# A graph layer on one core: five whole groups of gathered rows brought by SyncE, a place transfer issued from ScalarE, and the rows of v laid out in the table's order

## The chip, the cores and the metric

The kernel runs on one core of one Trainium2 chip. The time is device microseconds of one execution; three runs of the kernel before gave a median of 1986.8 us. Five engines work side by side and meet at semaphores: TensorE (PE, matmul), VectorE (DVE), ScalarE (ACT), GpSimd (POOL) and SyncE (SP). SP and ACT can issue direct DMA transfers, whose addresses may come out of a register; POOL issues the indirect ones, which take a column of 128 row numbers and bring 128 rows.

## The reference

For 6250 nodes with 64 features and 200000 edges sorted by target node `dst`:

```python
h   = relu(layernorm(x))
p1  = tanh(h @ pp_W1 + pp_b1) @ pp_W2 + pp_b2
e   = concat([p1[src], p1[dst]]) @ pi_W1 + pi_b1      # per edge
e   = ((e @ pi_W2 + pi_b2) @ pi_W3).reshape(E, 64, 8)
i1  = einsum('ecb,eb->ec', e, edge_attr)
i1  = tanh(i1 @ ii_W1 + ii_b1) @ ii_W2 + ii_b2
out = x + segment_sum(i1, dst, num_segments=6250)
```

Since nothing nonlinear stands between `p1` and the einsum, the kernel keeps two tables in DRAM: `u_tab` (a row of 64 float32 per node, for the side of `src`) and `v_tab` (a row of 3 x 64 bfloat16 per node, three parts whose sum is the float32 row, for the side of `dst`).

## The kernel before

The edges are cut into 391 groups (`NG`) of 512: four tiles of 128 edges; the last group, 390, holds 320 edges. After a prologue of about 70 us that makes the tables, every engine walks the groups in the same order, one pass per group, a few passes apart from each other.

- **PE** sums both sides for the group (`newest()`, line 1423): `sum_v` (line 1346) multiplies a one-hot matrix by a window of `v_tab`, and `place_rows` (line 1362) adds the gathered rows of u. Then it spreads the edge features (line 1371), multiplies (line 1379), transposes (line 1386) and adds up by target (line 1474), each for a group one to three passes older. The first 32 passes and the last 30 odd are written out; the passes between run in loops of 8, cut around each group that SP brings.
- **POOL** gathers the rows of u (line 568), four indirect transfers for a group, for groups 7 to 390 without those in `BY_SP`. For groups up to 31 there is a buffer each. From group 40 on it reuses 8 buffers (`UR`), so group g waits until pass g - 8 has used its rows (`s_ready`).
- **SP** has in each pass g (line 470): a wait until pass g - 4 has made its one-hot matrix and `load_loc(g)` (line 415), the places of the edges in their window, broadcast to 126 partitions, 126 KB; a wait until pass g - 4 is summed and the window of v (line 479), 42 table rows of 3 x 64 values, 15.8 KB, to 126 partitions, at a register address; every 16th pass the next source numbers and edge features; and in a stretch of passes `fetch_rows`, four single rows of u of 256 B at register addresses (line 440), for which it first reads four row numbers into registers (line 436). Every 8th pass it reads eight window starts into registers (line 472), with a bounds check on each. Three passes before the group is due, `place_fetched` (line 448) copies the staged rows to the place where PE takes them, in four transfers.
- **ACT** copies the sums out (`make_s`, line 756, four instructions), then does the tanh (line 744) and a copy (line 747) for the group two passes older (`make_t`).
- **DVE** makes the one-hot matrices (lines 1051 and 1094) and the products (line 987).

`BY_SP` names the groups that SP brings, the pass in which it begins, and over how many passes (one partition of four rows a pass):

```python
BY_SP = [(135, 4, P), (263, 132, P), (NG - 1, 260, PART)]
```

So SP brings groups 135, 263 and 390, 1344 rows, in passes 4 to 339. A window row of v for node n and part w lies on partition 42 w + n (`n w d -> w n d`), and the one-hot matrix compares with `iota_p`, which holds the partition modulo 42.

Of the kernel before, what the change touches and what calls it, by code (L numbers as in the profile page):

```python
# [8 lines left out]
def program(nc, x, src, dst, edge_attr, pp_W1, pp_b1, pp_W2, pp_b2, pi_W1, pi_b1, pi_W2, pi_b2, pi_W3,  # L9
# [6 lines left out]
    P = 128  # L16
# [59 lines left out]
    UNITS = [(k, min(2, XG - k)) for k in range(0, XG, 2)]  # L76
    EARLY_V = 4

    BY_SP = [(135, 4, P), (263, 132, P), (NG - 1, 260, PART)]

    assert EPP * NP == EARLY and LPP * NP == N - EARLY and LPP == 10 and Y_STEP + 4 * BATCHES < NG + 4
    assert NP * NPP == N and PART * TILES + FULL * GE == E and F == FC * P and NG <= PIECE * PIECES
# [4 lines left out]
    with ctx:  # L87
# [17 lines left out]
        ident = sb("ident", [P, P])  # L105
        ident_b = sb("ident_b", [P, P], bf16)
        iota_f = sb("iota_f", [P, BW])
        iota_i = sb("iota_i", [P, 2], i32)
        iota_p = sb("iota_p", [P, 3])
        iota_8 = sb("iota_8", [P, 1])  # L110
        spread = sb("spread", [P, NB, D], bf16)
        g_sb = sb("g_sb", [P, FC, D])
# [4 lines left out]

        u_rows = sb("u_rows", [P, UR, TILES, D])
        sp_stage = sb("sp_stage", [P, 2, TILES, D])
        sp_idx = sb("sp_idx", [P, len(BY_SP) * TILES], i32)  # L120
        v_win = sb("v_win", [3 * W, VR, D], bf16)
        loc_bc = sb("loc_bc", [P, VR, GE], bf16)
        hot_t = sb("hot_t", [3 * W, 2, GE], bf16)
# [201 lines left out]
        def has(g):  # L325
            return 0 <= g < NG
# [8 lines left out]
        def _(sp):  # L335
# [90 lines left out]
            oe = out[0:EARLY, :].rearrange("(p i) d -> p (i d)", i=EPP)  # L426

            def load_sp_idx():
                for k, (g, _, n) in enumerate(BY_SP):
                    sp.dma_start(sp_idx[0:n, k * TILES:(k + 1) * TILES],  # L430
                                 src[g * GE:g * GE + n * TILES].rearrange("(p j) -> p j", j=TILES)
                                 ).then_inc(sp_idx_in, 16)

            def fetch_rows(k, p):

                _, at = nc.values_load_multi_w_load_instructions(
                    sp_idx[p:p + 1, k * TILES:(k + 1) * TILES], engines=[mybir.EngineType.SP], min_val=0, max_val=N - 1,
                    skip_runtime_bounds_check_because="src names nodes of x")
                for j in range(TILES):
                    sp.dma_start(sp_stage[p:p + 1, k % 2, j, :], u_tab[bass.ds(at[j], 1), :]  # L440
                                 ).then_inc(sp_rows_in[k], 16)

            def place_fetched(k):

                g, _, n = BY_SP[k]
                sp.wait_ge(sp_rows_in[k], 16 * TILES * n)
                for j in range(TILES):
                    sp.dma_start(u_rows[:, g % UR, j, :], sp_stage[:, k % 2, j, :]).then_inc(fetched[k], 16)

            def store_early(lo, hi):  # L450
                cols = slice(lo * D, hi * D)
# [12 lines left out]
            with sp.If(is_fast):  # L464
                store_v()
                for g in range(VR):
                    load_loc(g)
                v_landed()
                load_sp_idx()
                for g in range(NG):  # L470
                    if g % 8 == 0:
                        _, starts = nc.values_load_multi_w_load_instructions(  # L472
                            base_row[0:1, g:min(g + 8, NG)], engines=[mybir.EngineType.SP], min_val=0, max_val=N - W)
                    start = starts[g % 8]
                    if g >= VR:
                        sp.wait_ge(hot_t_ready, g - VR + 1)
                        load_loc(g)
                        sp.wait_ge(s_ready, g - VR + 1)
                    sp.dma_start(v_win[:, g % VR, :], v_tab[bass.ds(start, W), :, :].rearrange("n w d -> w n d")
                                 ).then_inc(v_in[g % VR], 16)  # L480
                    k = g // PIECE + 2
                    if g % PIECE == 0 and k < PIECES:
                        if k >= LD:
                            sp.wait_ge(part1, k - LD + 1)
                        load_src(k)
                        load_basis(k)
                    if g == (PIECES - 2) * PIECE:
                        load_last()
                    if g == PIECE // 2:
                        load_x()  # L490
                    if g == BY_SP[0][1]:
                        sp.wait_ge(sp_idx_in, 16 * len(BY_SP))
                    for k, (of, first_at, n) in enumerate(BY_SP):
                        if k >= 2 and g == first_at:
                            sp.wait_ge(s_ready, BY_SP[k - 2][0] + 1)
                        if 0 <= g - first_at < n:
                            fetch_rows(k, g - first_at)
                        if g == of - 3:
                            place_fetched(k)
                    if g == NG - 6:  # L500
                        sp.wait_ge(y_ready, 4)
                        store_early(0, 4 * SLICE)
                store_rest()
# [20 lines left out]
        def _(pool):  # L524
# [31 lines left out]
            with pool.If(is_fast):  # L556
                pool.wait_ge(u_stored, 32 * NC)
                pool.wait_ge(ld[0], ld_count(0))
                for g in range(XG, NG):
                    k = g // PIECE  # L560
                    if g % PIECE == 0:
                        pool.wait_ge(ld[k % LD], ld_count(k))
                    if g in [of for of, _, _ in BY_SP]:
                        continue
                    if g >= AHEAD + UR:
                        pool.wait_ge(s_ready, g - UR + 1)
                    for j in range(TILES):
                        pool.indirect_dma_start(  # L568
                            out=u_rows[:, g % UR, j, :] if g >= AHEAD else first_u[:, g - XG, j, :],
                            out_offset=None, in_=u_tab[:, :],  # L570
                            in_offset=bass.IndirectOffsetOnAxis(
                                ap=src_e[:, g * TILES + j:g * TILES + j + 1].bitcast(u32), axis=0),
                        ).then_inc(u_in[g % UR] if g >= AHEAD else first_u_in[g - XG], 16)
# [20 lines left out]
        def _(act):  # L594
# [155 lines left out]
            def copy_st(r):  # L750
# [6 lines left out]
                            "p (q a e) -> p q a e", q=2, a=TILES), ACT.Identity, bias=s_bias[part, 0:1])  # L757
                return last

            def make_s(n):  # L760
                act.wait_ge(s_ready, n + 1)
                if has(n - 2):
                    act.wait_ge(o_ready, n - 1)
                copy_st(n % 2).then_inc(st_ready, 1)
# [16 lines left out]
            with act.If(is_fast):  # L781
                zero_upper()
                root_rows()
                place_columns()
                zero_lower()
                relu_rows(0)
                for k in range(1, len(UNITS)):
                    relu_rows(k)
                    tanh_rows(k - 1)
                tanh_rows(len(UNITS) - 1)  # L790
                for n in STEPS:
                    if has(n) and n < TURN:
                        make_s(n)
                    if has(n - 2):
                        make_t(n - 2)
                    if has(n) and n >= TURN:
                        make_s(n)
                store_rest()
# [15 lines left out]
        def _(dve):  # L814
# [61 lines left out]
            norm(4)  # L876
            dve.wait_ge(consts, 1)
            nc.vector.tensor_copy(ident_b[:], ident[:])
            nc.vector.tensor_copy(iota_p[:, 0:1], iota_i[:, 0:1])
            nc.vector.tensor_scalar(iota_i[:, 1:2], iota_i[:, 0:1], NB - 1, None, ALU.bitwise_and)  # L880
            dve.drain()
            for k in (1, 2):
                nc.vector.tensor_scalar(iota_p[:, k:k + 1], iota_p[:, 0:1], float(k * W), float(W), ALU.is_ge,
                                        ALU.mult)
            nc.vector.tensor_copy(iota_8[:], iota_i[:, 1:2])
            dve.drain()
            nc.vector.tensor_tensor(iota_p[:, 1:2], iota_p[:, 1:2], iota_p[:, 2:3], ALU.add)

            u_copy(0)
            dve.wait_ge(rows_in, 48)  # L890
# [16 lines left out]
            nc.vector.tensor_tensor(iota_p[:, 0:1], iota_p[:, 0:1], iota_p[:, 1:2], ALU.subtract)  # L907
# [276 lines left out]
        def _(pe):  # L1184
# [226 lines left out]
            skipped = [of for of, _, _ in BY_SP]  # L1411

            def step(n, u, first, last_pass, g=None, fetched_pass=False, gone=(0,) * UN):

# [8 lines left out]
                def newest():  # L1423
# [10 lines left out]
                        place_rows(first_u[:, g - XG, :, :], False).then_inc(s_ready, 1)  # L1434
                    else:
                        if fetched_pass and n + u in skipped:
                            pe.wait_ge(fetched[skipped.index(n + u)], 16 * TILES)
# [45 lines left out]
            with pe.If(is_fast):  # L1483
# [9 lines left out]
                    step(g - g % UN, g % UN, g < UN, False, g)  # L1493
                gone = [0] * UN
                at = AHEAD
                for of in skipped[:-1]:
                    with pe.Fori(at, of // UN * UN, UN) as n:
                        for u in range(UN):
                            step(n, u, False, False, gone=gone)
# [5 lines left out]
                with pe.Fori(at, LOOP_END, UN) as n:  # L1505
                    for u in range(UN):
                        step(n, u, False, False, gone=gone)
                for n in range(LOOP_END, NG + 5, UN):
                    for u in range(UN):
                        step(n, u, False, True, fetched_pass=True, gone=gone)  # L1510
                pe.wait_ge(acc_done, NG)
                y_late()
            with pe.Else():
# [48 lines left out]
```

## Time and profile before

| what | value |
|---|---|
| median of 3 runs (lowest to highest) | 1986.8 us (1985.95 to 1989.17) |
| the profiled execution's own time | 1983.09 us |
| its span, first to last instruction | 1981.2 us |
| busy PE, POOL, DVE, ACT | 1733.1, 1479.1, 1449.0, 1109.5 us |
| mean granted TensorE clock | 0.963 |

The profile is of one execution. Its span is 1.9 us shorter than its own time and its time is 3.7 us below the median. A busy time does not count the issuing of DMA transfers, so SP has none; what SP does is read from the timeline of its queue. POOL's gathers count as busy for about 0.94 us each, with 0.3 us from one to the next.

### The profile page before, as it was taken

The numbers are of one execution on the slowest core, as the hardware profiler recorded it, in microseconds if no ns is written. First come the engines' busy times: TensorE is split into PE (matmuls) and PEld (weight loads), VectorE is DVE, ScalarE is ACT, GpSimd is POOL, SyncE is SP. The second block draws the span as 40 slices with busy tenths as digits, with TensorE's granted clock in tenths as the row PEclk, the third lists the DMA queues.
The fourth block names the chain that finished last, engine by engine and source line by source line (L and its number), as shares of the span: only waits on it lengthen the run. The fifth ranks groups of instructions, "written<-read, shape, count | busy, mean of one in ns | idle before, by whom it ended". The sixth has DMA issues, their size and how long they took to land.

```text
span 1981.2 us, 58993 instructions
## 1 busy us (share of the span) xinstructions
PE 1733.1 (87%) x20012; PEld 1134.5 (57%) x20012; DVE 1449.0 (73%) x1939; ACT 1109.5 (56%) x2419; POOL 1479.1 (75%) x1569
## 2 busy tenths in 40 slices
PE   7699999989988898888888888888888888888998
PEld 6466566655555555555555555555555555555666
DVE  7688778877677777677777777677777767777766
ACT  5666656655555555555555555555555555555554
POOL 7777777777777777777777777777777777777773
PEclk9799999999899999999999999899999999999999
DMA  6543333333333332332333323333233233332331
GB/s 141 115 82 62 67 67 64 61 65 66 58 63 58 62 66 56 63 62 56 62 55 61 62 56 60 61 63 64 55 63 62 56 59 62 59 59 54 59 71 44
DMA packets 266170, 127.83 MB, mean 65 GB/s; under 512 B 188169, under 2 KB 238328, under 8 KB 265864
## 3 DMA queue, kind: packets, MB, share of 16 engines
q1 hardware_dynamic: 214767, 74.86, 17.9%
q0 software_dynamic: 49664, 50.96, 15.4%
q14 instruction: 134, 1.10, 0.2%
q8 instruction: 47, 0.77, 0.2%
q10 hardware_dynamic: 1558, 0.15, 0.1%
HBM read 119.42 MB, written 6.00 MB: 63 GB/s over the span
## 4 chain that ended last, share of the span: by engine, by line
POOL 62%; issue 21%; PE 11%; ACT 2%; DMA 1%; SPq 1%; DVE 1%; ACTq 0%; DVEq 0%; POOLq 0%
POOL u_rows L568 62%; PE bank L1379 5%; PE bank L1474 1%; PE bank L1362 1%; DMA loc_bc<-loc_tab 1%; PE bank L1386 1%; PE spread_ps L1371 1%; DVE o_sb L987 1%; PE bank L1346 1%; ACT st_sb L756 0%; SPq L472 0%; SPq L440 0%; PE spread_ps L1208 0%; PE bank L1356 0%; DMA v_tab<-acc_all 0%
## 5 line engine op out<-in xcount | busy, mean ns | idle before, releaser
L568 POOL DMA_INDIRECT u_rows<-u_tab,src_e x1424 | 1352.4, 950 | 434.1 <-issue 433.1
L987 DVE TENSOR_TENSOR o_sb<-st_sb,spread_ps 128x2048 f32<-128x2048 f32 x391 | 892.9, 2284 | 365.0 <-PE spread_ps L1371 346.8
L756 ACT ACTIVATE st_sb<-bank,s_bias 64x256 f32<-64x256 f32 x1564 | 734.3, 469 | 438.0 <-PE bank L1362 406.9
L1379 PE MATMUL bank<-o_sb,g_sb 128*64 128x256 f32 x6256 | 807.0, 403 | 1.0 <-DVE o_sb L987 0.8
L1379 PEld LDWEIGHTS bank<-o_sb,g_sb 128*64 128x64 f32 x6256 | 433.5, 143 | 232.9 <-issue 36.7
L1362 PE MATMUL bank<-ident,u_rows 128*128 128x128 f32 x1436 | 259.3, 304 | 191.9 <-DMA u_rows<-u_tab,src_e 191.0
L1051 DVE TENSOR_TENSOR hot_t<-loc_bc,bank 126x512 bf16<-126x512 bf16 x391 | 268.8, 688 | 144.0 <-PE bank L1474 59.7
L1362 PEld LDWEIGHTS bank<-ident,u_rows 128*128 128x128 f32 x1436 | 189.8, 192 | 240.5 <-DMA u_rows<-u_tab,src_e 228.0
L1474 PEld LDWEIGHTS bank<-hot,t_sb 128*65 128x65 f32 x3128 | 216.1, 139 | 158.6 <-issue 150.6
L744 ACT ACTIVATE tt_sb<-bank,z_bias 128x256 f32<-128x256 f32 x391 | 185.4, 474 | 175.1 <-PE bank L1379 174.4
L1474 PE MATMUL bank<-hot,t_sb 128*65 128x42 f32 x3128 | 262.8, 235 | 9.1 <-DVE acc_all L1100 8.6
L747 ACT COPY t_sb<-bank 128x256 f32<-128x256 f32 x391 | 146.5, 375 | 221.8 <-PE bank L1386 218.1
L1386 PE MATMUL bank<-ident,tt_sb 128*128 128x128 f32 x782 | 170.4, 300 | 0.6 <-ACT tt_sb L744 0.6
L1371 PE MATMUL spread_ps<-bt_sb,spread 24*128 24x128 bf16 x6256 | 161.0, 221 | 5.0 <-DVE o_sb L987 4.8
L1346 PE MATMUL bank<-hot_t,v_win 126*64 126x128 bf16 x1564 | 118.4, 231 | 12.0 <-issue 7.7
L1094 DVE TENSOR_TENSOR hot<-loc_e,bank 128x168 f32<-128x168 f32 x391 | 125.9, 322 | 0.0
L1371 PEld LDWEIGHTS spread_ps<-bt_sb,spread 24*128 24x128 bf16 x6256 | 92.6, 94 | 54.1 <-issue 6.4
L568 POOL DMA_INDIRECT basis<-u_tab,src_e x100 | 96.4, 964 | 31.9 <-issue 30.2
L1346 PEld LDWEIGHTS bank<-hot_t,v_win 126*64 126x64 bf16 x1564 | 56.1, 108 | 79.1 <-issue 78.5
L1386 PEld LDWEIGHTS bank<-ident,tt_sb 128*128 128x128 f32 x782 | 79.7, 142 | 35.5 <-ACT tt_sb L744 1.4
L1100 DVE TENSOR_TENSOR acc_all<-acc_all,bank 65x42 f32 x391 | 72.9, 186 | 3.5 <-PE bank L1474 3.5
L1035 DVE STREAM_TRANSPOSE bt_sb<-b_parts 128x512 bf16<-128x512 bf16 x98 | 68.5, 699 | 0.0
(148 smaller groups left out, 353.3 us busy)
## 6 DMA issues: line engine op xcount, KB each, us to landing
loc_bc<-loc_tab SPq DMA_DIRECT2D x391, 126.0 KB
u_rows<-u_tab,src_e POOLq DMA_INDIRECT x1424
sp_stage<-u_tab SPq DMA_DIRECT2D x1344, 0.2 KB
v_win<-v_tab SPq DMA_DIRECT2D x391, 15.8 KB
basis<-edge_attr SPq DMA_DIRECT2D x24, 256.0 KB, 4.2
v_tab<-acc_all SPq DMA_DIRECT2D x6, 336.0 KB
basis<-u_tab,src_e POOLq DMA_INDIRECT x100, 2.7
u_tab<-basis SPq DMA_DIRECT2D x6, 224.0 KB
```

The source lines that it names most:

```text
L568: pool.indirect_dma_start(out=u_rows[:, g % UR, j, :] if g >= AHEAD else first_u[:, g - XG, j, :], out_offset=None, in_=u_tab[:, :], in_of ...
L744: return nc.scalar.activation(tt_sb[:, r, :], z_ps, ACT.Tanh, bias=z_bias[:, 0:1])
L747: return nc.scalar.copy(t_sb[:, r, :, 0:D].rearrange("p (h q) c -> p q h c", h=2), t_ps.rearrange("p (q h c) -> p q h c", q=2, h=2))
L756: last = nc.scalar.activation(tiles[h * D:(h + 1) * D, j], s_ps[part].rearrange("p (q a e) -> p q a e", q=2, a=TILES), ACT.Identity, bias= ...
L987: return nc.vector.tensor_tensor(o_sb[:, r, :, :].rearrange("p c (j e) -> p j c e", j=TILES), st_sb[:, r, :].rearrange("p (j e) -> p j e", ...
L1051: nc.vector.tensor_tensor(hot_t[:, g % 2, :], loc_bc[0:3 * W, g % VR, :], pick_ps.to_broadcast([3 * W, GE]), ALU.is_equal).then_inc(hot_t_ ...
L1346: nc.tensor.matmul(s_ps[TWICE[j], q * P:(q + 1) * P].rearrange("k (a e) -> k a e", a=TILES), v_win[:, u % VR, :], hot_t[:, u % 2, :].rearr ...
L1362: last = nc.tensor.matmul(s_ps[:, q * P:(q + 1) * P], rows[:, 2 * q:2 * q + 2, :].rearrange("p j k -> p (j k)"), ident[:], start=alone and ...
L1371: last = nc.tensor.matmul(spread_ps[:, a, c * P:(c + 1) * P], spread[q, 2 * c:2 * c + 2, :].rearrange("p b k -> p (b k)"), bt_sb[q, r, :], ...
L1379: last = nc.tensor.matmul(z_ps[h * D:(h + 1) * D, 0:2 * P], g_sb[:, c, :], o_sb[:, r, c, 2 * h * P:(2 * h + 2) * P], start=(c == 0), stop= ...
L1386: last = nc.tensor.transpose(t_ps[:, q * P:(q + 1) * P], tt_sb[:, r, q * P:(q + 1) * P], ident[:])
L1474: last = nc.tensor.matmul(seg_ps, t_sb[:, (u - 3) % 2, j, :], hot[:, (u - 3) % HR, j, :], start=(j == 0), stop=(j == TILES - 1))
```

## The change

SP brings five whole groups, 83, 157, 231, 305 and 380, seven rows a pass, each over 74 passes (4 to 77, 78 to 151 and so on to 373). The row numbers of a group lie in one partition and are read eight at a time. The copy to the place where PE takes them is one transfer. POOL gathers the 320-edge last group, which SP brought before. `load_loc` moves from SP's queue to ACT's, behind `make_s`; ACT issues it for the group four passes on. The window of v lands in the order of the table (partition 3 n + w), so that its source is one run of rows, and `iota_p` holds the partition divided by 3. The bounds check on the window starts is left out. PE's loops are cut around four groups instead of two.

```diff
-    BY_SP = [(135, 4, P), (263, 132, P), (NG - 1, 260, PART)]
+    ROWS = 7
+    BY_SP = [(83, 4), (157, 78), (231, 152), (305, 226), (380, 300)]
+    AT_ONCE = 8
...
-        sp_idx = sb("sp_idx", [P, len(BY_SP) * TILES], i32)
+        sp_idx = sb("sp_idx", [1, len(BY_SP) * GE], i32)
...
             def load_sp_idx():
-                for k, (g, _, n) in enumerate(BY_SP):
-                    sp.dma_start(sp_idx[0:n, k * TILES:(k + 1) * TILES],
-                                 src[g * GE:g * GE + n * TILES].rearrange("(p j) -> p j", j=TILES)
+                for k, (g, _) in enumerate(BY_SP):
+                    sp.dma_start(sp_idx[0:1, k * GE:(k + 1) * GE], row(src[g * GE:(g + 1) * GE])
                                  ).then_inc(sp_idx_in, 16)
-            def fetch_rows(k, p):
-
-                _, at = nc.values_load_multi_w_load_instructions(
-                    sp_idx[p:p + 1, k * TILES:(k + 1) * TILES], engines=[mybir.EngineType.SP], min_val=0, max_val=N - 1,
-                    skip_runtime_bounds_check_because="src names nodes of x")
-                for j in range(TILES):
-                    sp.dma_start(sp_stage[p:p + 1, k % 2, j, :], u_tab[bass.ds(at[j], 1), :]
+            def fetch_rows(k, rows, at):
+
+                for r in rows:
+                    p, j = divmod(r, TILES)
+                    if r % AT_ONCE == 0:
+                        _, at = nc.values_load_multi_w_load_instructions(
+                            sp_idx[0:1, k * GE + r:k * GE + r + AT_ONCE], engines=[mybir.EngineType.SP], min_val=0,
+                            max_val=N - 1, skip_runtime_bounds_check_because="src names nodes of x")
+                    sp.dma_start(sp_stage[p:p + 1, k % 2, j, :], u_tab[bass.ds(at[r % AT_ONCE], 1), :]
                                  ).then_inc(sp_rows_in[k], 16)
+                return at
             def place_fetched(k):
-                g, _, n = BY_SP[k]
-                sp.wait_ge(sp_rows_in[k], 16 * TILES * n)
-                for j in range(TILES):
-                    sp.dma_start(u_rows[:, g % UR, j, :], sp_stage[:, k % 2, j, :]).then_inc(fetched[k], 16)
+                g, _ = BY_SP[k]
+                sp.wait_ge(sp_rows_in[k], 16 * GE)
+                sp.dma_start(u_rows[:, g % UR, :, :], sp_stage[:, k % 2, :, :]).then_inc(fetched[k], 16)
...
                         _, starts = nc.values_load_multi_w_load_instructions(
-                            base_row[0:1, g:min(g + 8, NG)], engines=[mybir.EngineType.SP], min_val=0, max_val=N - W)
+                            base_row[0:1, g:min(g + 8, NG)], engines=[mybir.EngineType.SP], min_val=0, max_val=N - W,
+                            skip_runtime_bounds_check_because="VectorE made them from dst and cut them at N - W")
                     start = starts[g % 8]
                     if g >= VR:
-                        sp.wait_ge(hot_t_ready, g - VR + 1)
-                        load_loc(g)
                         sp.wait_ge(s_ready, g - VR + 1)
-                    sp.dma_start(v_win[:, g % VR, :], v_tab[bass.ds(start, W), :, :].rearrange("n w d -> w n d")
+                    sp.dma_start(v_win[:, g % VR, :], v_tab[bass.ds(start, W), :, :].rearrange("n w d -> (n w) d")
                                  ).then_inc(v_in[g % VR], 16)
...
-                        if 0 <= g - first_at < n:
-                            fetch_rows(k, g - first_at)
+                        if first_at <= g:
+                            at = fetch_rows(k, range(ROWS * (g - first_at), min(ROWS * (g - first_at + 1), GE)), at)
...
+            def load_loc(g):
+                act.wait_ge(hot_t_ready, g - VR + 1)
+                act.dma_start(loc_bc[0:3 * W, g % VR, :], loc_tab[g:g + 1, :].to_broadcast([3 * W, GE])
+                              ).then_inc(loc_in[g % VR], 16)
...
                 for n in STEPS:
                     if has(n) and n < TURN:
                         make_s(n)
+                    if has(n + VR):
+                        load_loc(n + VR)
                     if has(n - 2):
                         make_t(n - 2)
...
-            nc.vector.tensor_copy(iota_p[:, 0:1], iota_i[:, 0:1])
             nc.vector.tensor_scalar(iota_i[:, 1:2], iota_i[:, 0:1], NB - 1, None, ALU.bitwise_and)
+            nc.vector.tensor_scalar(iota_i[:, 2:3], iota_i[:, 0:1], 171, None, ALU.mult)
             dve.drain()
-            for k in (1, 2):
-                nc.vector.tensor_scalar(iota_p[:, k:k + 1], iota_p[:, 0:1], float(k * W), float(W), ALU.is_ge,
-                                        ALU.mult)
+            nc.vector.tensor_scalar(iota_i[:, 0:1], iota_i[:, 2:3], 9, None, ALU.logical_shift_right)
...
-                for of in skipped[:-1]:
+                for of in [of for of in skipped if of < LOOP_END]:
                     with pe.Fori(at, of // UN * UN, UN) as n:
```

## Rows read from the trace of the kernel before

**Rows 1.** The page's part 4: the chain that ended last, by engine.

```profile
POOL 62%; issue 21%; PE 11%; ACT 2%; DMA 1%; SPq 1%; DVE 1%; ACTq 0%; DVEq 0%; POOLq 0%
```

**Rows 2.** Line 568: duration ns min/median/max, first and last start; idle until; landing.

```profile
L568 POOL DMA_INDIRECT u_rows<-u_tab,src_e x1424: 940/944/1532, 169.2 to 1954.5; - x178
L568 POOL DMA_INDIRECT basis<-u_tab,src_e x100: 940/944/1365, 42.4 to 168.0; - x100
...
  PE bank L1362: 0.9, 3
...
DMA to landing us min/median/max: 2.4/2.7/4.7
```

**Rows 3.** The chain that ended last, 1840 to 1982 us: start, length, what.

```profile
1919.51 4.69 DMA u_rows<-u_tab,src_e
...
1965.41 0.66 PE bank L1362 x4
```

**Rows 4.** Timeline of SP's queue, 140 to 165 us: start, length, line, transfer.

```profile
140.66 1.49 SPq L440 DMA_DIRECT2D sp_stage<-u_tab  x4
142.20 0.32 SPq L415 DMA_DIRECT2D loc_bc<-loc_tab  x1
142.71 0.75 SPq L479 DMA_DIRECT2D v_win<-v_tab  x1
144.50 1.50 SPq L440 DMA_DIRECT2D sp_stage<-u_tab  x4
...
160.32 1.52 SPq L440 DMA_DIRECT2D sp_stage<-u_tab  x4
164.76 0.35 SPq L415 DMA_DIRECT2D loc_bc<-loc_tab  x1
```

**Rows 5.** SP's instructions by line, whole span: duration ns min/median/max.

```profile
L440 SPq DMA_DIRECT2D sp_stage<-u_tab x1344: 224/225/465, 75.0 to 1691.6; - x192
L436 SPq TENSOR_LOAD <-sp_idx x336: 497/814/923, 74.0 to 1689.4; - x168
L472 SPq TENSOR_LOAD <-base_row x49: 689/783/1445, 60.6 to 1910.3; - x49
L479 SPq DMA_DIRECT2D v_win<-v_tab x391: 722/749/936, 64.0 to 1945.2; - x196
L415 SPq DMA_DIRECT2D loc_bc<-loc_tab x391: 311/320/1253, 55.5 to 1941.6; - x196
L448 SPq DMA_DIRECT2D u_rows<-sp_stage x12: 555/601/610, 658.1 to 1934.9; - x12
```

**Rows 6.** Waits of SP's queue, whole span: us in total, times, longest.

```profile
SPq L479 <- PE bank L1362: 294.7, 190, 5.1
```

**Rows 7.** Timeline of SP's queue, 60 to 240 us: the windows of passes 4, 17, 33.

```profile
73.22 0.76 SPq L479 DMA_DIRECT2D v_win<-v_tab  x1
...
134.98 0.78 SPq L479 DMA_DIRECT2D v_win<-v_tab  x1
...
205.11 0.77 SPq L479 DMA_DIRECT2D v_win<-v_tab  x1
```

**Rows 8.** Timelines of PE (passes 3 and 33) and POOL (group 41 begins).

```profile
84.85 0.30 PE L1346 MATMUL bank<-hot_t,v_win 126*64 126x128 bf16 x4
...
209.83 0.30 PE L1346 MATMUL bank<-hot_t,v_win 126*64 126x128 bf16 x4
...
214.17 0.94 POOL L568 DMA_INDIRECT u_rows<-u_tab,src_e  x1 [0.30 <-issue]
```

**Rows 9.** ACT and DVE near 701 us; line 1082 on DVE's queue; a transfer issued by ACT.

```profile
700.53 1.92 ACT L756 ACTIVATE st_sb<-bank,s_bias 64x256 f32<-64x256 f32 x4 [0.50 <-PE bank L1362]
702.75 0.47 ACT L744 ACTIVATE tt_sb<-bank,z_bias 128x256 f32<-128x256 f32 x1 [0.31 <-PE bank L1379]
...
701.12 2.29 DVE L987 TENSOR_TENSOR o_sb<-st_sb,spread_ps 128x2048 f32<-128x2048 f32 x1 [0.80 <-PE spread_ps L1371]
...
L1082 DVEq TENSOR_LOAD <-base_row x1: 320/320/320, 701.1 to 701.1; - x1
...
L602 ACTq DMA_DIRECT2D wraw<-L_gnn_pi_W x1: 665/665/665, 1.9 to 1.9; - x1
```

More of the change, by code:

```diff
@@ L107, in program @@
         iota_f = sb("iota_f", [P, BW])
-        iota_i = sb("iota_i", [P, 2], i32)
-        iota_p = sb("iota_p", [P, 3])
+        iota_i = sb("iota_i", [P, 3], i32)
+        iota_p = sb("iota_p", [P, 1])
         iota_8 = sb("iota_8", [P, 1])
@@ L469, in _ @@
                 load_sp_idx()
+                at = None
                 for g in range(NG):
@@ L492, in _ @@
                         sp.wait_ge(sp_idx_in, 16 * len(BY_SP))
-                    for k, (of, first_at, n) in enumerate(BY_SP):
+                    for k, (of, first_at) in enumerate(BY_SP):
                         if k >= 2 and g == first_at:
                             sp.wait_ge(s_ready, BY_SP[k - 2][0] + 1)
-                        if 0 <= g - first_at < n:
-                            fetch_rows(k, g - first_at)
+                        if first_at <= g:
+                            at = fetch_rows(k, range(ROWS * (g - first_at), min(ROWS * (g - first_at + 1), GE)), at)
                         if g == of - 3:
@@ L560, in _ @@
                     k = g // PIECE
+                    if g == FULL:
+                        pool.wait_ge(last_in, 32)
                     if g % PIECE == 0:
                         pool.wait_ge(ld[k % LD], ld_count(k))
-                    if g in [of for of, _, _ in BY_SP]:
+                    if g in [of for of, _ in BY_SP]:
                         continue
@@ L878, in _ @@
             nc.vector.tensor_copy(ident_b[:], ident[:])
-            nc.vector.tensor_copy(iota_p[:, 0:1], iota_i[:, 0:1])
             nc.vector.tensor_scalar(iota_i[:, 1:2], iota_i[:, 0:1], NB - 1, None, ALU.bitwise_and)
+            nc.vector.tensor_scalar(iota_i[:, 2:3], iota_i[:, 0:1], 171, None, ALU.mult)
             dve.drain()
-            for k in (1, 2):
-                nc.vector.tensor_scalar(iota_p[:, k:k + 1], iota_p[:, 0:1], float(k * W), float(W), ALU.is_ge,
-                                        ALU.mult)
+            nc.vector.tensor_scalar(iota_i[:, 0:1], iota_i[:, 2:3], 9, None, ALU.logical_shift_right)
             nc.vector.tensor_copy(iota_8[:], iota_i[:, 1:2])
             dve.drain()
-            nc.vector.tensor_tensor(iota_p[:, 1:2], iota_p[:, 1:2], iota_p[:, 2:3], ALU.add)
+            nc.vector.tensor_copy(iota_p[:], iota_i[:, 0:1])
             u_copy(0)
@@ L906, in _ @@
                                     ).then_inc(rows_done, 1)
-            nc.vector.tensor_tensor(iota_p[:, 0:1], iota_p[:, 0:1], iota_p[:, 1:2], ALU.subtract)
             u_copy(3)
@@ L1409, in y_late @@
                     last.then_inc(y_ps, 1)
-            skipped = [of for of, _, _ in BY_SP]
+            skipped = [of for of, _ in BY_SP]
             def step(n, u, first, last_pass, g=None, fetched_pass=False, gone=(0,) * UN):
@@ L1436, in newest @@
                         if fetched_pass and n + u in skipped:
-                            pe.wait_ge(fetched[skipped.index(n + u)], 16 * TILES)
+                            pe.wait_ge(fetched[skipped.index(n + u)], 16)
                         else:
@@ L1504, in _ @@
                     at += UN
-                with pe.Fori(at, LOOP_END, UN) as n:
-                    for u in range(UN):
-                        step(n, u, False, False, gone=gone)
+                if at < LOOP_END:
+                    with pe.Fori(at, LOOP_END, UN) as n:
+                        for u in range(UN):
+                            step(n, u, False, False, gone=gone)
                 for n in range(LOOP_END, NG + 5, UN):
@@ L1510, in _ @@
                         step(n, u, False, True, fetched_pass=True, gone=gone)
+                        if n + u in skipped:
+                            gone[u] += 1
                 pe.wait_ge(acc_done, NG)
```

## The prediction, made before the changed kernel had run

> **What bounds the kernel now.** I read the chain that ended last first, because the shares of busy time name PE (1733 us) while PE spends much of its time waiting. The chain goes to POOL for 62%, and most of its "issue" is the 0.3 us between two of POOL's gathers [rows 1]. The view of line 568 tells why: 1524 gathers, the first at 42.4 and the last at 1954.5 us, so one every (1954.5 - 42.4) / 1523 = 1.2555 us, and all of POOL's waiting for PE is 0.9 us [rows 2]. POOL never rests from its first gather to its last. A group costs it 4 x 1.2555 = 5.02 us; PE, where nothing holds it, needs 4.1 us a pass (30 passes from pass 3 to pass 33 took 125 us [rows 8], some of them already late). So POOL's early lead over PE is eaten up, and from then on PE runs at POOL's pace.
>
> The end of the chain must be read apart. POOL's last gather, of group 389, is not on it: the chain leaves POOL at the gather that starts at 1919.51, 28 gathers before the last, which is the last one of group 382; PE then runs eight more passes by itself, and the end comes 61.7 us after that gather [rows 2, 3].
>
> SP is the second limit. Its pass is read off its queue's timeline [rows 4, 5]: the four rows take 1.49 us from first start to last end with 0.225 each, so one row every 0.42 us. From the end of the v transfer to the first row it is 1.04 us; without the reading of the row numbers it would be the 0.20 between two rows, so reading costs 0.84. The places cost 0.32 + 0.055, v 0.19 + 0.75. Sum: 4 x 0.42 + 0.84 + 0.375 + 0.94 = 3.84. From v of pass 17 to v of pass 33 are 70.13 us, 4.38 a pass [rows 7]; the 0.54 more is two readings of the window starts, the 16-pass transfers and small delays. Over the whole run SP still waits 294.7 us for PE [rows 6].
>
> **What each part costs or gives.**
>
> *POOL.* Five whole groups leave it instead of two whole ones and the last, so it gathers 379 groups instead of 381: 8 x 1.2555 = 10.0 us less in all. The path, however, leaves POOL at group 382. Before that group two had been skipped, now five: 12 gathers less, 15.1 us, so the gather at 1919.51 moves to 1904.4. With the same 61.7 us behind it the span ends at 1966.1. A check from the other side: group 390 is now POOL's. Its last gather starts 32 gathers after 1904.4, at 1944.6; 2.7 us to landing [rows 2] gives 1947.3, and from the sum of the last group (1965.41) to the end are 15.8 us [rows 3]: 1963. So POOL's own last gather would just not be the later one. The landing on the chain took 4.69 where 2.7 is usual; with a usual one the end comes 2 us earlier. 1963 to 1970 is what this part leaves open; I take 1966.
>
> *SP's pass.* Rows: 512 / 74 = 6.92 a pass x 0.42 = 2.91. Reading eight numbers is not shown for these numbers, but eight window starts take 0.783 in one instruction against 0.814 for four row numbers [rows 5], so a reading costs the same 0.84, now 64 in 74 passes: 0.73. The places leave. The starts without their bounds check: every eighth pass 2.9 us go by between row and places (161.84 to 164.76), of which the reading is 0.78; the checks cost 2.05 each eighth pass, 0.26 a pass, and the 0.54 of other work becomes 0.28. The copy to the place is one transfer instead of four of 0.6 and costs nothing beside that.
>
> The v transfer is the open price. Its new form (126 destination partitions, one run of rows in DRAM) is not in the trace. Upper bound: the old 0.749. Lower bound: the places' transfer, which goes to the same 126 partitions with eight times the bytes in 0.320 [rows 5]. I take 0.32, the row nearest in shape, and keep 0.75. The pass is then 2.91 + 0.73 + 0.19 + 0.32 + 0.28 = 4.43, or 4.86 with the old price. The trace shows two transfers to 126 partitions with more than twofold different issue times [rows 5]. The Trainium skill (DMA: Bandwidth & Descriptors, Why a DMA increments its semaphore by 16 and not by 1) says that the engines a transfer runs on are the largest number up to 16 that divides both sides' slowest dimension: by it the old v, whose source has 3 in front, runs on 3 and the new one on 14, as the places do. By that rule the sum is the one with 0.32; a reader who sets the rule aside has 4.43 to 4.86.
>
> Does 4.43 suffice? In the long run yes: POOL's pace is 5.02 x 73 / 74 = 4.95 a pass. The same by totals: 1216 more rows x 0.42 = +511, 387 places gone -145, bounds checks -100, readings -13, v -168 gives +85 us out of 294.7 of slack; with the old v +253, which leaves some 42.
>
> The beginning is tighter, because there PE runs ahead of 4.95 and POOL's 8 buffers tie it to PE: group 41 may start when pass 33 is summed. It started at 214.17; pass 33 began at 209.83 and its sum takes about 0.95, so 3.4 us were spare [rows 8]. How late is v of pass 33 now? From pass 4 to 33, 29 passes: rows +3 x 0.42 x 29 = +36.5; readings -0.125 x 0.84 x 29 = -3.0; places -10.9; v -12.5; four bounds checks -8.2: +1.9 us, so it is issued at 207.0 instead of 205.1. With 0.32 and a landing of 2.7 (the gathers'; v's own is not shown) pass 33 can begin at 210.0, as before. No stall. With the old v it is issued at 219.5, pass 33 is summed near 223.9, and POOL loses 9.7 us.
>
> *ACT.* It issues 387 transfers that SP issued at 0.32 and that ACT could issue at up to 0.67 [rows 9]. The wait in front is met already: the sums that `make_s` has just copied needed the same one-hot matrix. I count it at nothing, since ACT's queue can issue while its four copies of 1.92 us run; the trace shows that for DVE, whose queue reads a window start at 701.1 while its 2.29 us product runs [rows 9]. If the cover is gone, the tanh, which idles 0.31 us for PE, comes 0.67 - 0.31 = 0.36 later, and PE's transposes with it. In exchange the places come from a queue that is not busy. This removes waits of DVE, but not on the path that sets the end.
>
> *The rest.* Two more transfers of row numbers (about 0.9 us on SP) stand ahead of pass 0, with 2 us of checks gone in the same place. DVE's constants are a few tiny instructions on either side. PE has 16 more passes written out, and the first 32, written out too, run at 4.1. I add nothing.
>
> **The sum.** The profiled execution's span becomes 1966.1 (15.1 less), its own time 1.9 more, 1968.0; the median of the runs lay 3.7 above the profiled time: 1971.7, say 1972 us, 0.7% less.
>
> **The rivals.**
>
> *A: v's issue stays at 0.75.* For: no row shows the new form. Against: the row of the places. POOL stalls 9.7 us early, SP at 4.86 stays just inside 4.95: 1971.7 + 9.7 = 1981, 0.3% faster. It bites from a v of 0.32 + 3.4 / 30 = 0.43 on.
>
> *B: ACT's issue is not hidden.* PE's free pass becomes 4.1 + 0.36; pass 33 begins at 84.85 + 30 x 4.46 = 218.7 and is summed at 219.6, so POOL stalls 5.4 us at group 41; the eleven passes from 380 to 390 add 4. 1971.7 + 9.4 = 1981. Against: DVE's row.
>
> *C, slower: the single rows choke.* SP sends 1.56 rows per us instead of 4 / 4.38 = 0.91, each a transfer of its own. If they back up, a row costs more than 0.42 and SP becomes the bound: pass 373 can begin no sooner than 73.2 + 369 s. POOL brings group 373 by 1904.4 - 8 x 5.02 = 1864, so s up to about 4.86 is free; the 15 us of gain are gone at 4.90, which is a row of 0.49. At 0.52 s is 5.12, which is (5.12 - 4.86) x 369 = 96 us over the forecast: 2068. Against: 1344 rows at a median of 225 ns, never over 465, four in a row at 0.42 [rows 5]. The skill's same page and section says that a transfer of one row runs on one engine, the lowest-numbered one, which speaks against 2560 of them; no row here shows which engine took them.
>
> *D: nothing gained at the end,* if PE, not POOL, sets the last passes from group 380 on. But it comes out of group 380 with one skipped group as lead and needs about 4.2 where POOL needs 5.02; that loses at most the 4 us up to 1970. The time would be 1976.
>
> **How the numbers follow.** Forecast 0.68 (1966 to 1977, with stalls of a few us inside it), A 0.11, B 0.11, C 0.08, the rest better than forecast. Within 0.2% (1982.8 to 1990.8) is about what a measurement of this kernel can tell from no change. A and B lie just below its edge, half of each in it. So faster 0.80, same 0.11, slower 0.09. The range is 1965 to 1985: it leaves out C and the dearer ends of A and B.
>
> **What would show it.** Line 440: 2560 rows at 225 ns, 0.42 apart. Line 479 near 0.32. SP's wait for PE near 210 us. POOL's last gather at 1944 to 1945 and its waiting for PE under 2 us; 5 to 10 us there is A or B. ACT's tanh still 0.3 us behind the copies where PE is free: else B. The chain leaving POOL in the last ten groups. The prediction is wrong if SP's queue stands on the chain after 300 us.

## The result, and the profile after

| | before | after |
|---|---|---|
| median of 4 runs (lowest to highest) | 1986.97 us (1985.95 to 1989.17) | 1971.34 us (1966.45 to 1973.25) |
| ratio to before, 95% interval | | 0.9916 [0.9896, 0.9937] |
| the profiled execution's own time; its span | 1983.09; 1981.2 us | 1972.48; 1970.7 us |
| mean granted TensorE clock | 0.963 | 0.969 |

The kernel is 0.8% faster, and the interval lies wholly below no change. The forecast was 1972. The span that it was built on was 1966.1, though, and the span is 1970.7: 4.6 us of the sum were missed. The median was taken to lie 3.7 us above the profiled execution's time, and this time it lies 1.1 below it. The two misses cancel by luck, so the close agreement of the totals says less than the agreement of the steps.

First the page's part 4 of the changed kernel, the chain that ended last, by engine [rows 1]:

```profile
POOL 55%; issue 21%; PE 11%; SPq 9%; DMA 1%; ACT 1%; DVE 0%; ACTq 0%; POOLq 0%; DVEq 0%
```

POOL still leads. SP's queue, at 1% before, has 9%. Now POOL's gathers, line 573 (duration ns min/median/max, first and last start; then idle until; landing) [rows 2]:

```profile
L573 POOL DMA_INDIRECT u_rows<-u_tab,src_e x1416: 943/947/1496, 169.7 to 1948.5; - x177
L573 POOL DMA_INDIRECT basis<-u_tab,src_e x100: 943/947/1452, 42.5 to 168.5; - x100
...
  PE bank L1371: 1.2, 4
...
DMA to landing us min/median/max: 2.4/2.9/5.0
```

1516 gathers instead of 1524, and again no rest: the waiting for PE is 1.2 us in four pieces, and each piece is no more than the 0.3 us that lie between any two gathers. The pace is (1948.5 - 42.5) / 1515 = 1.2581 us instead of 1.2555.

Instructions of SP and ACT by line, whole span (duration ns min/median/max) [rows 5]:

```profile
L443 SPq DMA_DIRECT2D sp_stage<-u_tab x2560: 224/228/2403, 74.9 to 1853.1; - x197
L440 SPq TENSOR_LOAD <-sp_idx x320: 687/783/949, 74.0 to 1848.4; - x160
L482 SPq DMA_DIRECT2D v_win<-v_tab x391: 321/322/1177, 63.0 to 1934.4; - x196
L451 SPq DMA_DIRECT2D u_rows<-sp_stage x5: 490/492/1099, 415.0 to 1872.2; - x5
L767 ACTq DMA_DIRECT2D loc_bc<-loc_tab x387: 313/314/636, 73.5 to 1934.3; - x194
```

The row kept its price. The window of v fell from 749 to 322 ns, the lower of the prediction's two bounds. Waits of SP's queue [rows 6]:

```profile
SPq L482 <- PE bank L1371: 207.8, 174, 6.1
```

The chain that ended last, from 200 to 446 us (start, length, what), around passes 33 and 34 and where POOL takes over [rows 7, 8]:

```profile
200.82 1.06 SPq L358
...
202.06 2.40 SPq L443
...
207.98 1.70 DMA v_win<-v_tab
...
209.91 0.30 PE bank L1355 x4
...
215.95 0.64 PE bank L1371 x4
...
437.39 3.27 DMA v_win<-v_tab
440.70 0.30 PE bank L1355 x4
441.00 0.66 PE bank L1371 x4
441.91 0.95 POOL u_rows L573
```

Up to 437 us SP's queue stands on the chain again and again, but nothing is lost there: v of pass 33 is issued at 207.98 and pass 33 begins at 209.91, 0.08 later than before, and POOL does not wait. Two of POOL's gathers, the first of group 42 and the first of group 87 (timeline of POOL; in brackets the idle time before):

```profile
220.29 0.95 POOL L573 DMA_INDIRECT u_rows<-u_tab,src_e  x1 [0.30 <-issue]
...
441.91 0.95 POOL L573 DMA_INDIRECT u_rows<-u_tab,src_e  x1 [0.30 <-PE bank L1371]
```

and the sum of pass 79 (timeline of PE; the passes are counted by their sums):

```profile
414.58 0.71 PE L1371 MATMUL bank<-ident,u_rows 128*128 128x128 f32 x4
```

Group 42 needs pass 34, which is summed at 215.95 + 0.64 = 216.59. With the usual 0.30 us between gathers it could have begun at 216.89, so 3.4 us were spare. That is the least of any group that reuses a buffer. Group 87 needs pass 79, summed at 415.29 at the latest, so 26 us were spare at 441.91. The page names PE as what released that gather only because the sum of a later pass, 85, ended inside the ordinary 0.3 us. So the link by which the chain comes from SP's queue to POOL is no delay, and the 9% do not say that SP's queue held anything up.

The chain at the end [rows 3]:

```profile
1893.40 3.64 DMA u_rows<-u_tab,src_e
1897.08 1.23 PE bank L1371 x4
...
1903.13 0.64 PE bank L1371 x4
...
1936.45 0.53 PE bank L1403 x7
...
1954.59 0.66 PE bank L1371 x4
```

The chain leaves POOL 44 gathers before the last, at group 378, not 382. PE then runs to the sum of group 390 in 57.5 us, 13 steps of 4.42 on average (12 groups and one step without a sum). In most of these steps it also transposes rows of the output (line 1403, 0.53 us).

### The profile page after: what moved, and what is told of

It is laid out like the page before. It is cut to its first block, busy times and chain, and to the rows that moved or that the text cites. A ratio compares the mean times of both kernels' runs of the same rounds, so it can differ in the third digit from the quotient of the medians.

```text
span 1970.7 us, 61801 instructions
## 1 busy us (share of the span) xinstructions
PE 1717.0 (87%) x20012; PEld 1125.7 (57%) x20012; DVE 1453.4 (74%) x1937; ACT 1109.4 (56%) x2419; POOL 1474.1 (75%) x1561
## 4 chain that ended last, share of the span: by engine, by line
POOL 55%; issue 21%; PE 11%; SPq 9%; DMA 1%; ACT 1%; DVE 0%; ACTq 0%; POOLq 0%; DVEq 0%
POOL u_rows L573 55%; SPq L443 6%; PE bank L1388 4%; SPq L440 2%; PE bank L1371 1%; PE bank L1483 1%; SPq L482 1%; PE bank L1395 1%; PE spread_ps L1380 1%; PE bank L1355 1%; DMA p<-L_gnn_pi_W 0%; DMA v_win<-v_tab 0%; PE spread_ps L1217 0%; DMA u_rows<-u_tab,src_e 0%; PE bank L1223 0%
## 5 line engine op out<-in xcount | busy, mean ns | idle before, releaser
L1388 PE MATMUL bank<-o_sb,g_sb 128*64 128x256 f32 x6256 | 792.4, 397 | 1.0 <-DVE o_sb L996 0.8
L1388 PEld LDWEIGHTS bank<-o_sb,g_sb 128*64 128x64 f32 x6256 | 427.3, 140 | 225.2 <-issue 23.9
```

Source lines behind the costliest of these rows:

```text
L1388: last = nc.tensor.matmul(z_ps[h * D:(h + 1) * D, 0:2 * P], g_sb[:, c, :], o_sb[:, r, c, 2 * h * P:(2 * h + 2) * P], start=(c == 0), stop= ...
```

## The experiments

Each diff is against the changed kernel. Every kernel computes the whole reference. The chips differed by up to 6 us in the kernel before, so kernels are compared by their ratio to it on the same chip; a time given behind a ratio is the ratio times 1986.97.

**e1: v's window in its old order, all else changed.**

```diff
-                    ... v_tab[bass.ds(start, W), :, :].rearrange("n w d -> (n w) d")
+                    ... v_tab[bass.ds(start, W), :, :].rearrange("n w d -> w n d")
```

The lines that make `iota_p` go back with it.

> The changed kernel with v's old order in SBUF (three parts of 42 partitions), all else as changed. The theory (POOL's gathers set the end as long as SP's pass stays below POOL's 4.95 us and POOL has 3 to 4 us to spare at group 41): v's issue goes back from 0.322 to 0.75, SP's pass from the measured 4.53 to 4.96, pass 33 comes some 12 us later, POOL waits 8 to 12 us for PE early on and SP's waiting for PE falls from 208 to about 40 us or less: 1980 to 1990 us. Rival, that the layout matters little because SP had slack anyway: under 1975. Rival, that the issue time hangs on the bytes and not on the pattern: v's issue stays near 0.32.

Measured: 1.009 [1.0073, 1.0107], 2004.9 us, slower than before. The expectation was missed. SP's windows of passes 4 and 373, the first and the last in which it brings rows (timeline of its queue):

```profile
69.97 0.73 SPq L482 DMA_DIRECT2D v_win<-v_tab  x1
...
1898.73 0.74 SPq L482 DMA_DIRECT2D v_win<-v_tab  x1
```

That is (1898.73 - 69.97) / 369 = 4.956 a pass, and from 240 us to the last row no window waits for PE. Its waits for a sum over the whole span, below, all lie after 1905 us:

```profile
SPq L482 <- PE bank L1374: 40.9, 13, 3.6
```

PE waits for these windows instead (waits of PE in e1), 181.8 us where the changed kernel has 8.9:

```profile
PE bank L1358 <- DMA v_win<-v_tab: 181.8, 189, 4.4
```

So SP sets the pace as long as it brings rows. The issue of v (median 757 ns) was as assumed; the pass around it is 0.10 longer than the 4.86 of the prediction. Rival A called that "just inside". By rival C's own formula a pass of 4.956 costs (4.956 - 4.86) x 369 = 35 us over the forecast: 2007, beside the 2004.9.

**e4: the rows alone.** Old order of v, the places on SP, the bounds checks kept: the edits of e1, e2 and e3 in one kernel.

> Only the five groups at seven rows a pass: v's old order, the places on SP and the checks kept. POOL has the same 8 gathers less than before. The theory: SP's pass is 2.91 + 0.73 + 0.375 + 0.94 + 0.54 + 0.1 = 5.6 us, SP becomes the bound up to pass 373: 73 + 369 x 5.6 + 98 for the rest = 2240 us, 2180 to 2260 with SP's waits near nothing. Rival, that POOL sets the end whatever SP does: 1971 to 1985.

Measured: 1.1291 [1.1269, 1.1314], 2243.5 us. Windows of passes 4 and 373, timeline of SP's queue:

```profile
73.10 0.76 SPq L483 DMA_DIRECT2D v_win<-v_tab  x1
...
2137.30 0.75 SPq L483 DMA_DIRECT2D v_win<-v_tab  x1
```

5.594 a pass; the formula gives 1971.7 + 0.734 x 369 = 2242.6. POOL waits 291.2 us for PE, and the chain has SP's queue for 71%. Without the relief of SP the five groups lose 13%.

**e2: the places back on SP.**

```diff
                     if g >= VR:
+                        sp.wait_ge(hot_t_ready, g - VR + 1)
+                        load_loc(g)
                         sp.wait_ge(s_ready, g - VR + 1)
...
-                    if has(n + VR):
-                        load_loc(n + VR)
```

> The changed kernel with the places' transfer back on SP, with its wait, all else as changed. The theory: SP's pass +0.37, 4.90 us; pass 33 comes 10 us later, POOL waits 6 to 8 us early, SP's slack falls from 208 to about 60 us: 1976 to 1984 us. Rival, that moving the places to ACT gave nothing since DVE waited only 44 us for them: 1971, POOL waits under 2 us.

Measured: 0.9982 [0.9973, 0.9992], 1983.4 us. **e3: the bounds checks kept**, without the last argument of the reading at line 476.

> The changed kernel with the bounds check on the window starts kept, all else as changed. The theory: 2.05 us more every eighth pass, 100 us in all out of 208 of slack, pass 33 some 8 us later of which 3.7 are spare: POOL waits 4 to 5 us, 1973 to 1979 us. Rival, that 0.26 us a pass is lost in the slack: 1971, POOL waits under 2 us.

Measured: 0.994 [0.9923, 0.9957], 1975.0 us. **e6: eight rows a pass**, `ROWS = 8`, same groups.

> The changed kernel with eight rows a pass instead of seven: the same five groups, the same 2560 rows, the same gathers, fetched in 64 passes of each 74, so that SP rests in the other ten. The theory, that the early tie counts and not the sum: SP's pass is 5.06 while it fetches, pass 33 comes 15 us later, POOL waits 9 to 13 us early, and SP is level with POOL's pace after that: 1980 to 1988 us. Rival, that only SP's total counts: 1971.

Measured: 0.9965 [0.9951, 0.9979], 1980.0 us. These three are read together. POOL's waiting for PE from 160 to 250 us (idle us, times), first e2:

```profile
  PE bank L1371: 16.6, 3
```

then e3:

```profile
  PE bank L1370: 6.3, 3
```

then e6:

```profile
  PE bank L1371: 9.4, 4
```

In the changed kernel there is no such line in this stretch; in e1 it has 13.1 us. Later, e2, e3 and e6 have only the ordinary 0.3 a time (e1 has up to 1.3). So the stall is where the prediction looked for it, at POOL's first reuse of its buffers, and nowhere else. In e3 it was somewhat larger than the 4 to 5 us expected. In e2, where 6 to 8 us were expected, it was more than twice that. The expectation priced only the longer pass of SP. But the places come late there too, behind SP's rows, and DVE waits for them (waits of DVE in e2), which it did for 44.1 us before and does not at all in the changed kernel:

```profile
DVE hot_t L1060 <- DMA loc_bc<-loc_tab: 344.0, 239, 5.2
```

How much of the 16.6 us is theirs was not taken apart. Against the changed kernel's 0.9916 the three lose 13, 5 and 10 us, about what POOL waits. (The interval of e3 overlaps that of the changed kernel, so there the 6.3 us of waiting are the firmer number.) SP's waiting over the whole span does not tell it. In e6:

```profile
SPq L482 <- PE bank L1371: 222.0, 61, 5.5
```

That is more slack than the changed kernel's 207.8, in a kernel that is 10 us slower: SP has it late, and POOL lost its time early.

**e5: two groups only, with all of SP's relief.**

```diff
-    ROWS = 7
-    BY_SP = [(83, 4), (157, 78), (231, 152), (305, 226), (380, 300)]
+    ROWS = 4
+    BY_SP = [(135, 4), (263, 132)]
```

> The changed kernel with only two groups, 135 and 263, brought by SP at four rows a pass; all that relieves SP stays. POOL gathers 382 groups, 12 gathers more than the changed kernel and 4 more than the kernel before. The theory, that only the number of gathers pays: 12 x 1.256 = 15 us more than the changed kernel, 1984 to 1990 us, though SP waits for PE over 400 us. Rival, that the relief of SP and the earlier places pay by themselves: under 1980.

Measured: 0.9989 [0.998, 0.9998], 14.5 us behind the changed kernel, where 12 gathers at 1.2555 make 15.1. SP waits 1027.5 us there:

```profile
SPq L482 <- PE bank L1371: 1027.5, 364, 5.9
```

With all that slack, the rest of the change, without fewer gathers ahead of the tail, moves the time by 0.1%. The gain is POOL's gathers.

**e7: ACT issues the places twice**, in two transfers of 63 partitions.

```diff
-                act.dma_start(loc_bc[0:3 * W, g % VR, :], loc_tab[g:g + 1, :].to_broadcast([3 * W, GE])
-                              ).then_inc(loc_in[g % VR], 16)
+                for half in (slice(0, 63), slice(63, 126)):
+                    act.dma_start(loc_bc[half, g % VR, :], loc_tab[g:g + 1, :].to_broadcast([63, GE])
+                                 ).then_inc(loc_in[g % VR], 16)
```

SP's four transfers ahead of the loop are cut likewise, and DVE waits for twice the count.

> The changed kernel with the places' transfer cut into two of 63 partitions, so that ACT issues twice as often with the same bytes. The theory, that ACT's queue issues while its copies run: two issues of 0.3 still fit beside 1.92 us, the tanh still starts 0.31 after the copies, PE's free pass stays 4.10: 1969 to 1974 us. Rival, that ACT's issue is on the path: PE's free pass 4.1 + 0.3 to 0.4, POOL waits 4 to 8 us: 1977 to 1982.

Measured: 0.991 [0.9889, 0.9931], no cost within the interval. Timeline of ACT in e7 near 131 us (start, length, engine, line; in brackets the idle time before):

```profile
130.55 0.47 ACT L762 ACTIVATE st_sb<-bank,s_bias 64x256 f32<-64x256 f32 x1 [0.50 <-PE bank L1373]
130.56 0.65 ACTq L769 DMA_DIRECT2D loc_bc<-loc_tab  x2
131.04 1.44 ACT L762 ACTIVATE st_sb<-bank,s_bias 64x256 f32<-64x256 f32 x3
132.78 0.48 ACT L750 ACTIVATE tt_sb<-bank,z_bias 128x256 f32<-128x256 f32 x1 [0.30 <-PE bank L1390]
```

The queue issues two transfers, 0.65 us, while the four copies run, and the tanh still idles 0.30 for PE, as before [rows 9]. PE's free passes take 4.10 us, in e7 as in the changed kernel (its sums begin at 224.76, 228.86 and 232.96 there).

**e8, e9, e11: six groups**, nine rows a pass. ACT issues v's windows too. The copy to the place comes from SP three passes ahead in e8, from ACT five passes ahead in e9 and e11.

```diff
-    ROWS = 7
-    BY_SP = [(83, 4), (157, 78), (231, 152), (305, 226), (380, 300)]
+    ROWS = 9
+    BY_SP = [(68, 0), (128, 57), (184, 114), (242, 171), (300, 228), (372, 285)]
...
+            def load_v(g):
...
+                act.wait_ge(s_ready, g - VR + 1)
+                act.dma_start(v_win[:, g % VR, :], v_tab[bass.ds(starts[(g - VR) % 8], W), :, :].rearrange(
+                    "n w d -> (n w) d")).then_inc(v_in[g % VR], 16)
```

> A version meant to go further: v's transfer moves to ACT's queue as well, so that no pass of PE hangs on SP's pace; SP brings six groups (68, 128, 184, 242, 300, 372) at nine rows a pass over 57 passes each, and waits for PE only at the 16-pass transfers and before a copy to its place. POOL gathers 378 groups, 4 gathers less than the changed kernel; the last skipped group is 372 instead of 380, so PE comes to the end with less of a tail behind POOL. The theory: 5 us from POOL and up to 3 from the tail, 1962 to 1968 us, with no wait of POOL for PE. Rival, that ACT's queue with places, v and window starts (0.32 + 0.5 + 0.1) delays the tanh: PE's free pass over 4.3, 1971 to 1980. Rival, that nine single rows back to back choke: row issues well over 0.23 and groups that come too late, over 1980.

Measured: 0.991 [0.9894, 0.9926], no clear gain over the changed kernel, so the expectation was missed. PE waited for five late copies (waits of PE in e8):

```profile
PE bank L1385 <- DMA u_rows<-sp_stage: 119.0, 5, 33.8
```

> The version with six groups, but the copy of the fetched rows to their place is issued by ACT in the pass five before the group, instead of by SP at the end of its own, late row of work. In the version before, PE waited 119 us in all for five of these copies, up to 34 us for one, because SP's queue came to them behind rows of the next group. The theory, that those late copies ate the gain: PE waits under 10 us for the copies, POOL does not wait for PE, POOL's 4 gathers (5 us) and 2 to 3 us of the tail come off the changed kernel: 0.4% less than it, a ratio to the kernel before of 0.986 to 0.989. Rival, that the rows themselves come too late: waits for the copies stay over 50 us, ratio 0.990 or more. Rival, that PE with its 4.1 us a pass and not POOL bounds the end by then: no late copies, and no gain, 0.991.

Measured: 0.9905 [0.9889, 0.9921]. The late copies are gone, but 0.986 to 0.989 was expected, and that was missed again; ACT waits once, 12.8 us, for the rows of group 68. e11 is e9 with group 74 in place of 68.

> The version with six groups and the copies issued by ACT, with its first group 74 instead of 68, so that ACT does not wait 12.8 us in pass 63 for SP's rows. The theory: POOL hardly waited there (1.8 us), so the wait cost little; 4 gathers less than the changed kernel, POOL's last gather 5 to 7 us earlier than in it, and 4 to 8 us less in the medians of the same chip: a ratio to the kernel before of 0.986 to 0.990. Rival, that single executions scatter by as much as the sixth group brings: not distinguishable from the changed kernel, 0.990 to 0.992.

Measured: 0.9906 [0.9891, 0.9921], as its rival said and not as the theory did; ACT waits for no rows.

**e10, e12: the changed kernel again**, on the chips of e9 and of e11.

> The changed kernel once more, to have it on the same chip and in the same rounds as the version with six groups: a ratio of 0.990 to 0.993 to the kernel before, POOL's last gather some 10 us earlier than there.

> The changed kernel once more, on the same chip and in the same rounds as the version with six groups: 0.990 to 0.993.

Measured: 0.9917 [0.9903, 0.9931] and 0.9917 [0.9904, 0.9931]. The changed kernel stands at 0.9916, 0.9917 and 0.9917, the six groups at 0.9905 and 0.9906, and the intervals overlap. Whether the sixth group gives anything stays open; it does not show the further 5 us that four gathers are worth.

## Why the prediction was right, and where it was not

**POOL is the bound, and 12 gathers ahead of the tail are the gain: right.** e5 puts them back and loses 14.5 us; all the rest of the change together leaves the kernel at 0.9989 of the time before.

**POOL's last gather, 1944.6 forecast, 1948.5 measured: mis-sized.** The step held POOL's pace at 1.2555. It was 1.2581, and 1515 x 0.0026 = 3.9 us is the whole miss. No wait makes it: the median gather took 947 ns instead of 944. The changed kernel itself ran at either median and at 1.2533 to 1.2581 a gather (last section), so the pace was a scatter that the range had to carry; an effect of the change on it is not shown.

**The end behind POOL: nearly right.** Forecast 1966.1 - 1944.6 = 21.5 us, measured 1970.7 - 1948.5 = 22.2. The chain was to leave POOL in the last ten groups; it left at group 378, with 12 groups to go. PE's steps there take 4.42, and 4.2 was assumed in rival D. D is therefore there in small: POOL's last rows land at about 1948.5 + 2.9 = 1951.4, and their sum begins at 1954.59, 3.2 us later, within the 4 us that D was allowed.

**v at 0.32: right, 0.322.** e1 shows that the order alone decides it: 757 ns for the same bytes in the old order. The Trainium skill (DMA: Bandwidth & Descriptors, Why a DMA increments its semaphore by 16 and not by 1) takes the engines from the largest number up to 16 that divides both sides' slowest dimension. The two times lie in the direction of that rule, but the section says nothing of issue times, and how many engines ran either transfer stands in no row. That the engines make the difference is not shown.

**SP's pass, 4.43: 0.10 too small.** From v of pass 17 to v of pass 33 it took (207.98 - 135.43) / 16 = 4.53, and in e1 it was 4.956 where 4.86 was worked out. The two excesses have different causes. Between passes 17 and 33 it is one row behind the edge features: 2.40 us, where no row took over 465 ns before; over 16 passes the 2.17 us more are 0.14 a pass, and the other work cost a little less than the 0.28 assumed. In e1 no row took over 1.14 us. Added up over SP's queue from 69.97 to 1898.73 us, its 2559 rows take 1117.7 us with the register work of each, 0.437 a row. The prediction had 0.42, from the spacing inside a run of four rows, and left out that the first row behind another instruction takes longer (0.274 against 0.225 us at 144.50 in the kernel before). 6.92 x 0.017 = 0.12 a pass, so the price of a row is the term that was mis-sized. In the changed kernel it cost nothing: pass 33's window was issued 1.0 us later than forecast, but it landed 1.70 us from the start of its issue where 0.32 + 2.7 was assumed.

**No stall at group 41: right, with 3.4 us to spare** (at group 42), about as much as in the kernel before. e2, e3 and e6 each make SP's early passes longer by more than that, and POOL stalls there at once, by 6 to 17 us.

**Rival A was mispriced: the one step that would have failed.** It gave 1981 with the old v, "0.3% faster"; e1 measured 0.9% slower. The error is e1's 0.10 a pass. The gap between the estimate 4.86 and POOL's 4.95 was treated as room, though rival C's line put the last free pass at 4.86 and the break-even at 4.90. So the issue time of v, which no row of before showed in its new form, decided the sign. Taking it from the places' row was right; pricing the other end was not.

**ACT's issue costs nothing: right.** e7 doubles it and finds the same within 4 us.

**C, the rows choke: no.** 2560 rows at a median of 228 ns. Its formula was the best tool of the prediction: with the measured pass it gives e1 and e4 within 3 us.

**SP's wait, about 210 us: right, 207.8,** though the count left the run's length as it was, and the span became 10.5 us shorter; part of the agreement is luck. SP's queue stands on the chain up to 437 us, past the 300 that was to prove the prediction wrong. That test was badly chosen: the chain reaches POOL there over a link that delayed nothing (26 us were spare). POOL's waiting was the right test.

## What to carry to other kernels

Work moved from the engine that sets the pace to a queue beside it paid in full here (14.5 us for 12 gathers), because that queue's pass stayed under the pace. Past the pace, every pass costs (e1, e4). Work out the queue's pass at the place where the two are tied most closely (here the first reuse of the buffers), not from its idle time over the whole run. An estimate that comes out within 2% of such a limit has not decided on which side it lies, so the price of its most uncertain term decides the sign. And a link of the chain is inferred: before it is read as a delay, look whether the work that it names was needed so early.

## What was unexpected of the hardware

The same gathers take a median of 944 or 947 ns from one execution to another: 944 in eleven of the fourteen traces and 947 in three. After and e10 have 947 and e12 has 944, with the same kernel. Over 1515 gathers the 3 ns are 4.5 us, about what a whole group is worth (5 us). As much again comes from single gathers of over 1 us (the fifth column has their number and by how much they exceed the median in all):

| execution | groups by SP | gathers | median ns | over 1 us: number, us | first to last start, us | per gather, us | span, us |
|---|---|---|---|---|---|---|---|
| after | 5 | 1516 | 947 | 53, 10.4 | 42.5 to 1948.5 | 1.2581 | 1970.7 |
| e10, same kernel | 5 | 1516 | 947 | 43, 8.9 | 41.8 to 1946.2 | 1.2570 | 1966.9 |
| e12, same kernel | 5 | 1516 | 944 | 39, 7.1 | 41.3 to 1940.1 | 1.2533 | 1961.0 |
| e9 | 6 | 1512 | 944 | 51, 11.6 | 41.3 to 1939.6 | 1.2563 | 1959.5 |
| e11 | 6 | 1512 | 947 | 50, 12.1 | 40.9 to 1943.0 | 1.2588 | 1965.0 |

What sets the level was not found, nor what makes the long gathers. e9 and e12 have the same median, and 4.5 us more of long gathers in e9 eat up nearly all of what its four gathers less should give. Whether the sixth group has a part in that is open: two traces of it are too few. It is why single profiles can't settle the sixth group.

The row of 2.40 us stands directly behind the transfer of the edge features, and it is the longest of its kind. In the changed kernel 16 rows begin within 0.2 us of the end of that issue; 15 of them take 0.68 to 2.40 us, with a median of 0.76. Where a reading of row numbers stands between the two, five times from 797 to 1115 us, the row takes 0.30. In the kernel before, a reading always stood there: the row near pass 33 began 0.77 us after the end of that issue (202.98 after 202.21) and took 0.30. In e6 a reading stands between them too, and 3 of 19 such rows still took 1.00 to 1.41 us. That the queue was still busy with that transfer is argued, not shown.

ACT's queue issues transfers beside ACT's running copies: 0.31 to 0.65 us a pass in 387 passes, at no cost that e7's interval shows.
